# One language-model tower on one core: a copy moved to VectorE, a sum to GpSimd, and normalized rows transposed ahead of the scores

## The reference

```python
x = word_emb[ids] + pos_emb[arange(128)] + type_emb[types]
h = gamma * (x - mu) / sqrt(var + 1e-12) + beta
a = layernorm(h)                                   # eps 1e-5
q, k, v = a @ Wq, a @ Wk, a @ Wv                   # 16 heads of 16
q, k = head_layernorm(q), head_layernorm(k)        # with weight and bias
p = softmax(where(causal, q k^T / 4, -inf))
h = h + (p v) @ Wo + bo
x2 = layernorm(h)
score = softmax(x2 @ gate^T); top 2 of score + bias, the weight is the score
h = h + sum over the two: (silu(xw @ w1[e]) * (xw @ w3[e])) @ w2[e],  xw = x2 * score
```

## Time and profile before

| | |
|---|---|
| runs, median | 545.32 us |
| the profiled execution | 545.62 us |
| its span | 543.8 us |
| granted TensorE clock, mean | 0.992 of full speed |
| TensorE busy | 501.2 us (92%) |
| VectorE busy | 291.9 us (54%) |
| ScalarE busy | 250.7 us (46%) |
| GpSimd busy | 286.2 us (53%) |

### The profile page before, as it was taken

One profiled execution on the slowest core, in us unless ns is written; L12 is line 12 of the kernel. 1 busy time (PEld: TensorE's weight loads), 2 busy tenths in 40 slices (PEclk: granted clock), 3 DMA queues, 4 the chain that ended last, 5 costly groups with the idle time before them and its releaser, 6 DMA issues.

```text
span 543.8 us, 13452 instructions
## 1 busy us (share of the span) xinstructions
PE 501.2 (92%) x4470; PEld 428.7 (79%) x4471; DVE 291.9 (54%) x759; ACT 250.7 (46%) x575; POOL 286.2 (53%) x532
## 2 busy tenths in 40 slices
PE   5877989998999888999999999999999999999991
PEld 2345666777776665499999999999999999999980
DVE  2778888889989887733333333333333333333330
ACT  1166788978997883243223322332233323332320
POOL 4678787677764675214543454345434454344432
PEclk9999999999999999999999999999999999999996
DMA  5007721101028672302212221122112221222221
GB/s 174 10 22 243 231 85 31 58 29 29 29 80 278 212 251 84 90 22 41 29 30 39 39 39 22 37 39 39 23 36 39 39 28 31 39 38 30 30 39 19
DMA packets 29962, 36.75 MB, mean 68 GB/s; under 512 B 8272, under 2 KB 23504, under 8 KB 29936
## 3 DMA queue, kind: packets, MB, share of 16 engines
q0 software_dynamic: 8352, 12.76, 13.8%
q1 hardware_dynamic: 20768, 22.61, 13.1%
q10 hardware_dynamic: 816, 1.06, 0.6%
HBM read 26.81 MB, written 9.50 MB: 67 GB/s over the span
## 4 chain that ended last, share of the span: by engine, by line
PE 79%; DVE 5%; POOL 5%; ACT 4%; issue 3%; DMA 2%; POOLq 0%; DVEq 0%; ACTq 0%
PE PS L1445 35%; PE PS L1456 18%; PE PS L1172 10%; PE PS L1296 5%; PE PS L1254 2%; PE PS L1395 2%; PE PS L1271 2%; DMA x_pair<-word_dram,idx 1%; PE PS L1180 1%; ACT work L628 1%; PE PS L1310 1%; PE PS L1243 1%; DVE nmax L879 1%; DMA out_dram<-x_pair,dst_c 1%; POOL arena L477 1%
## 5 line engine op out<-in xcount | busy, mean ns | idle before, releaser
L1445 PEld LDWEIGHTS PS<-work,arena 128*128 128x128 f32 x1716 | 197.6, 192 | 2.3 <-ACT work L744 0.4
L1445 PE MATMUL PS<-work,arena 128*128 128x128 f32 x1716 | 198.0, 275 | 0.0
L750 ACT ACTIVATE work<-PS 128x768 f32<-128x768 f32 x39 | 31.6, 810 | 197.2 <-PE PS L1445 197.2
L1456 PE MATMUL PS<-w_sb,work 128*128 x468 | 107.6, 379 | 0.7 <-DVE x_pair L1147 0.7
L1139 DVE TENSOR_TENSOR work<-work,PS 128x640 f32<-128x640 f32 x39 | 32.0, 821 | 138.0 <-ACT work L750 138.0
L1456 PEld LDWEIGHTS PS<-w_sb,work 128*128 128x128 f32 x468 | 85.9, 190 | 11.2 <-issue 1.1
L572 POOL DMA_INDIRECT out_dram<-x_pair,dst_c x39 | 79.2, 2030 | 21.9 <-POOL dst_c L571 20.5
L571 POOL COPY dst_c<-dest_i 128x1 int32 (+1 forms) x39 | 7.1, 183 | 138.7 <-DVE x_pair L1147 136.5
L628 ACT ACTIVATE work<-PS,nmax 128x128 f32<-128x128 f32 x256 | 72.0, 401 | 3.7 <-DVE nmax L879 3.7
L740 ACT ACTIVATE arena<-w_sb 128x1408 f32 x40 | 55.1, 1379 | 12.0 <-DVE er_i L1115 9.0
L1172 PE MATMUL PS<-ident,work 128*128 128x128 f32 x336 | 54.8, 276 | 1.8 <-ACT work L628 1.8
(11 more groups left out here) (172 smaller groups left out, 618.8 us busy)
## 6 DMA issues: line engine op xcount, KB each, us to landing
w_sb<-w_dram SPq DMA_DIRECT2D x16, 640.0 KB, 5.6
w_sb<-w_dram SPq DMA_DIRECT2D x8, 704.0 KB, 4.5
x_rows<-x SPq DMA_DIRECT2D x16, 128.0 KB, 2.3
out_dram<-arena SPq DMA_DIRECT2D x16, 128.0 KB, 2.4
w_sb<-w_dram SPq DMA_DIRECT2D x16, 64.0 KB, 6.2
w_sb<-w_qkv_dram ACTq DMA_DIRECT2D x1, 768.0 KB, 8.2
work<-x_rows,src_c POOLq DMA_INDIRECT x41, 2.8
out_dram<-x_pair,dst_c POOLq DMA_INDIRECT x39
```

Source lines behind the costliest of these rows:

```text
L1445: last = n.matmul(up_ps[p][:, i, c, :], ws[p][:, k, at:at + P], xT_sb[p][:, k, :], start=(k == 0), stop=(k == DK - 1))
L1456: last = n.matmul(PS[:, 7, 0:D], hT_sb[p][:, i, :], w2_sb[:, bass.ds(e, 1), i, :], start=(i == 0), stop=(i == FK - 1))
```

## The change

- ScalarE's copy of the first bank of transposed probabilities goes to VectorE (`transposed_first`) for t of 2 and more, behind the keys. It has a semaphore of its own, `probsT0_ready`; those who wait for the copies wait for both.
- The sum of word rows and `x_base` goes from VectorE to GpSimd (`x_sum`) for sequences of 5 and more, ahead of the gather. VectorE's statistics of that sum move behind the `x2` normalization for t of 2 and more.
- The transposes of `a_n` for sequences of 4 and more go from behind the scores of the step t (for t + 2) to the end of the step (for t + 3), into the second half of VY_BANK, behind the mask banks and ahead of the next scores. ScalarE's copy `aT` goes to the end of its step. `outputs` waits for `aT` only at t = 1, and for `var_f` in each step.
- The keys of the sequences 0 to 2 are written by ScalarE, ahead of its queries, no longer by VectorE.

```diff
@@ gpsimd
+                def x_sum(u, q, n):
+                    pool.wait_ge(x_base_ready, u + 1)
+                    pool.wait_ge(gathered[q], 16 * (n + 1))
+                    g.tensor_tensor(x_in[q], x_in[q], x_base, ALU.add).then_inc(x_summed, 1)
+                    if valid(t + 4) and not at_step(t, 0):
+                        x_sum(t + 4, p, half(4))
                     if valid(t + 5):
                         gather(t + 5, 1 - p, link)
@@ scalar
                 def queries_out(u):
-                    act.wait_ge(k_ready, u + 1)
+                    if isinstance(u, int) and u < KEYS_BY_ACT:
+                        act.wait_ge(qk_ps, u + 1)
+                    else:
+                        act.wait_ge(k_ready, u + 1)
...
+                    if isinstance(u, int) and u < KEYS_BY_ACT:
+                        a.activation(kT.rearrange("p b s -> p (b s)"), PS[:, T_BANK, D:2 * D], ACT.Identity,
+                                     scale=cols_sb[:, 4:5], bias=cols_sb[:, 5:6]).then_inc(k_ready, 1)
                 u = t + 2
-                if valid(u):
+                if valid(u) and early_rows(u):
                     act.wait_ge(aT_ps, u + 1)
...
-                if valid(t):
+                if at_step(t, 1):
                     transposed(0)
...
                     transposed(3)
+                u = t + 3
+                if valid(u) and valid(t) and not early_rows(u):
+                    act.wait_ge(aT_ps, u + 1)
+                    act.wait_ge(v_done, u - 1)
+                    a.activation(aT[1 - p].rearrange("p k s -> p (k s)"), PS[:, VY_BANK, D:2 * D],
+                                 ACT.Copy).then_inc(aT_ready, 1)
@@ vector
+                def transposed_first():
+                    dve.wait_ge(probsT_ps, RG * t + 1)
+                    wait(dve, pv_done, t)
+                    v.tensor_copy(probsT[:, 0:512], PS[:, 0, :]).then_inc(probsT0_ready, 1)
...
                     keys_out(t + 1)
+                if valid(t) and not at_step(t, 0) and not at_step(t, 1):
+                    transposed_first()
...
-                if valid(t + 4) and valid(t):
+                if valid(t + 4) and valid(t) and (at_step(t, 0) or at_step(t, 1)):
                     sum_rows(t + 4, p, half(4))
...
                     normalize(x2[p][:, :], row(u), 2).then_inc(x2_ready, 1)
+                if valid(t + 4) and valid(t) and not at_step(t, 0) and not at_step(t, 1):
+                    sum_rows(t + 4, p, half(4))
@@ tensor
                 def outputs(u):
-                    pe.wait_ge(probsT_ready, RG * u + RG)
+                    pe.wait_ge(probsT0_ready, u + 1)
+                    pe.wait_ge(probsT_ready, (RG - 1) * u + RG - 1)
                     pe.wait_ge(v_ready, u + 1)
-                    wait(pe, aT_ready, u + 4)
+                    if at_step(t, 1):
+                        pe.wait_ge(aT_ready, u + 4)
...
                 u = t + 2
-                if valid(u):
+                if valid(u) and early_rows(u):
                     pe.wait_ge(a_ready, u + 1)
-                    wait(pe, var_f, u - 3)
                     wait(pe, aT_ready, u)
                     transposes(a_n, DK, O_BANK).then_inc(aT_ps, 1)
...
                     mask_banks(t + 1)
+                u = t + 3
+                if valid(u) and not early_rows(u):
+                    pe.wait_ge(a_ready, u + 1)
+                    pe.wait_ge(aT_ready, u)
+                    pe.wait_ge(v_ready, u - 1)
+                    transposes(a_n, DK, VY_BANK, D).then_inc(aT_ps, 1)
```

More of the change, by code:

```diff
@@ L224, in build_tower @@
         s_done, max_done, exp_done = sem("s_done"), sem("max_done"), sem("exp_done")
-        probsT_ps, probsT_ready, pv_done, o_ready = (
-            sem("probsT_ps"), sem("probsT_ready"), sem("pv_done"), sem("o_ready"))
+        probsT_ps, probsT_ready, probsT0_ready, pv_done, o_ready = (
+            sem("probsT_ps"), sem("probsT_ready"), sem("probsT0_ready"), sem("pv_done"), sem("o_ready"))
         o_raw_ready, o_back, oT_ps, oT_ready, wo_done = (
@@ L277, in build_tower, with early_rows @@
         EARLY = 5
+        KEYS_BY_ACT = 3
+        def early_rows(u):
+            return isinstance(u, int) and u < 4
         def valid(t):
@@ L634, in transposed @@
                     wait(act, pv_done, t)
-                    a.activation(probsT[:, r * 512:(r + 1) * 512], PS[:, T_BANK if r == RG - 1 else r, :], ACT.Copy).then_inc(probsT_ready, 1)
+                    a.activation(probsT[:, r * 512:(r + 1) * 512], PS[:, T_BANK if r == RG - 1 else r, :],
+                                 ACT.Copy).then_inc(probsT0_ready if r == 0 else probsT_ready, 1)
                 def x2_out(u):
@@ L684, in step @@
                     transposed(1)
+                    queries_out(1)
                     transposed(2)
-                    queries_out(1)
                     squares(2)
@@ L920, in sum_rows @@
                                                ALU.add).then_inc(x_base_ready, 1)
-                    dve.wait_ge(x_base_ready, u + 1)
-                    dve.wait_ge(gathered[q], 16 * (n + 1))
-                    v.tensor_tensor(x, x, x_base, ALU.add).then_inc(x_summed, 1)
+                    if isinstance(u, int) and u < EARLY:
+                        dve.wait_ge(x_base_ready, u + 1)
+                        dve.wait_ge(gathered[q], 16 * (n + 1))
+                        v.tensor_tensor(x, x, x_base, ALU.add).then_inc(x_summed, 1)
                     dve.wait_ge(x_summed, u + 1)
@@ L962, in step @@
                     normalize_a(2)
-                    keys_out(0)
                     squared_sums(1)
@@ L979, in step @@
                     first_norm(3)
-                    keys_out(1)
                     stats(link, row(3), 1, var_a)
@@ L1191, in rank @@
                     pe.wait_ge(v_ready, B - 2)
+                    pe.wait_ge(aT_ready, B)
                     n.matmul(ranks0, upper[:, :], chosen[:, s0:s1, :], start=True, stop=False, skip_group_check=True)
@@ L1235, in mask_banks @@
                     pe.wait_ge(exp_done, RG * u)
-                    pe.wait_ge(probsT_ready, RG * u - 1)
+                    pe.wait_ge(probsT0_ready, u)
+                    pe.wait_ge(probsT_ready, (RG - 1) * u - 1)
                     n.matmul(PS[:, RG - 2, 0:E], identb[:, :], mask[:, 0:E], start=True, stop=True)
@@ L1259, in outputs @@
                 def outputs(u):
-                    pe.wait_ge(probsT_ready, RG * u + RG)
+                    pe.wait_ge(probsT0_ready, u + 1)
+                    pe.wait_ge(probsT_ready, (RG - 1) * u + RG - 1)
                     pe.wait_ge(v_ready, u + 1)
-                    wait(pe, aT_ready, u + 4)
+                    if at_step(t, 1):
+                        pe.wait_ge(aT_ready, u + 4)
                     if at_step(t, B):
                         pe.wait_ge(added, 1)
-                    elif edge and t + 2 >= B:
+                    else:
                         wait(pe, var_f, u)
@@ L1346, in step @@
                     if not edge or t > 0:
-                        pe.wait_ge(probsT_ready, RG * t)
+                        pe.wait_ge(probsT_ready, (RG - 1) * t)
                     transposes(qkn, 2 * DK, T_BANK).then_inc(qk_ps, 1)
```

1 line of the change is left out of this document (removed).

## The result

The changed kernel takes 549.33 us (median of its runs, 548.15 to 549.48) against 545.38 us for the kernel before on the same chip (545.27 to 545.5): ratio 1.0065, 95% interval 1.0052 to 1.0078. It is slower by 3.9 us. The forecast was 546.4, 1.1 above the kernel before, with a range up to 548.8. So the sign of the forecast was right and its size was wrong. The profiled execution took 549.19 us, 3.57 more than the one of before.

What follows compares the result with a forecast made beforehand. TensorE's own work was taken to bound the steps, with VectorE's normalization late next. Terms 1.4 - 0.5 - 0.3 - 1.8 + 1.1 + 0.3 + 0.4 + 0.5 = +1.1 us gave 546.4; range 543.8 to 548.8.

Steps and rivals of the forecast that it cites:

- The old wait: TensorE idle ahead of `outputs` behind ScalarE's copy of the transposed rows, 0.65 us a step; the change takes it out.
- the head of a step: Scores to query transposes: gains only 0.09 us, not 0.65, because VectorE's normalization is late next; nine heads, -0.8.
- The even-odd difference that I put on `x2`: t = 5, 7, 9: transposes of `x2` start late behind VectorE; `x2` now comes earlier, 3 x 0.1, -0.3 us.
- The start: From t = -1: ScalarE makes the keys, VectorE's sum of squares starts at 29.85 instead of 31.71; -1.8 us.
- t = 1: GpSimd does its power before the sum, so VectorE's statistics start 1.12 later, ahead of the awaited division; +1.1 us.
- The issue-gap term: Scores of t = 5, 7, 9 after the loop's jump: queued transposes cover 0.15 us each, -0.5 in all.
- tails: Step ends: the two transposes behind the mask banks add their issue, 0.22 us each; ten tails, +2.2.
- The end: t = 12 and t = 14: VectorE has no idle time for the copy's 0.60 us; +0.4 and +0.5.
- Rival 2: Transposes at the step's end cost nothing, covered by mask banks and issue gap; 544.7 us; chance 0.25.
- Rival 3: The wait ahead of `outputs` goes as a whole, which needs a shorter query chain; 540 to 542 us; chance 0.1.
- Rival 1: GpSimd's sum holds VectorE, sign: statistics over 6.0 us behind the scores; +1.6, 548.0 us; chance 0.25.
- The 1.6 us that I worked out from it: t = 4 to 11: if sum and `x2` normalization exclude each other, TensorE waits 0.2 us in each step, +1.6.

Runs made afterwards that it cites:

- sum_back: The changed kernel with the sum of word rows and base row back on VectorE, where its statistics now stand: 550.05 us, ratio 1.0089 to the kernel before.
- after_hole: The changed kernel with the a_n transposes straight behind `outputs` and ScalarE's copy of them between the first and second exponentials: 547.25 us, ratio 1.0022 to the kernel before.
- copy_back: The changed kernel with the copy of the first bank back on ScalarE in all steps: 547.58 us, ratio 1.0035 to the kernel before.
- place_only: The kernel before with only the new place of the a_n transposes, behind the mask banks: 548.44 us, ratio 1.0055 to the kernel before.
- mix: after_hole with the first copy on ScalarE from t = 12 and the sum of t = 1 on VectorE: 545.44 us, ratio 0.9994 to the kernel before.
- keys_only: The kernel before with the keys of sequences 0 to 2 written by ScalarE, nothing else: 544.29 us, ratio 0.9975 to the kernel before.
- mix_order: mix with VectorE's normalization of queries and keys ahead of the second maxima: 545.89 us, ratio 1.0006 to the kernel before.

## Why the prediction was wrong in size

**What went as forecast.** The old wait goes and one for VectorE's normalization stands in its place; the head of a step gains 0.10 in the even steps and 0 in the odd ones (forecast 0.10 and 0.08, 0.09 on the mean). In the odd ones the chain of VectorE ends 3.05 us behind the scores in both kernels (135.41 + 0.68 less 133.04; 134.93 less 131.88), and TensorE follows 0.13 behind it, as before, not the 0.05 that I took. The even-odd difference that I put on `x2` is there (7.1 to 6.98). The start: the first scores come at 29.16 (forecast 29.2), and VectorE's sum of squares, by the rows of the kernel after, at 29.90 (forecast 29.85):

```profile
27.55 0.56 ACT L681 ACTIVATE w_sb<-PS,cols_sb 128x256 f32<-128x256 f32 x1 [1.64 <-PE PS L1205]
...
29.27 0.60 ACT L691 ACTIVATE w_sb<-PS 128x512 f32<-128x512 f32 x1 [0.24 <-PE PS L1333]
```

```profile
29.90 0.69 DVE L916 TENSOR_REDUCE ss<-w_sb 128x32 f32<-128x512 f32 x1 [0.15 <-ACT w_sb L691]
```

The scores of t = 1 come 1.76 earlier (39.73 in place of 41.49), forecast 1.8. At t = 1 VectorE waits for GpSimd's sum:

```profile
49.41 0.43 DVE L823 BATCH_NORM_STATS2 st<-x_pair 128x6 f32<-128x256 f32 x1 [2.75 <-POOL x_pair L481]
```

The statistics start 9.68 us behind that step's scores where they stood at 8.54 (50.03), 1.14 later, forecast 1.12. The step takes 1.52 more than before, forecast 1.1 and a tail of 0.22; sum_back gives 1.07 of it back. TensorE's wait for the division there, forecast at 1.8, is 1.7 us in after_hole; in the kernel after a slower projection lies over most of it (last section).

**The step that failed** is "the two transposes added behind the mask banks lengthen it by their issue: [...] I take 0.22". It is 0.37, inside the bound of 0.44, which I had left aside for the row nearest in kind. That row, 138.68 to 138.92 in the earlier trace rows, is of a pair among other full-array work. The row that stands at the place itself is the other one there, masks to scores, 142.28 to 142.64: 0.36 us, of which the weight load is busy for 0.12 (the row at 142.28 above) and pauses for the rest. So a pause was to be seen at that place, and by the runs there are two of them once the pair stands there. The issue-gap term itself held: of the 0.24 to 0.29 that the jump costs before, the pair hides 0.12 to 0.18, and I took 0.15; it only comes off 0.37. Over t = 4 to 11: tails 2.5 in place of 1.3 with the gap in it, heads -0.5 in place of -0.7, `x2` -0.4 in place of -0.3. These make 1.4 of the 2.5 us that the profiled sum is off.

**The end** is most of the rest, 0.7. I let t = 12 absorb its tail in the late division (+0.4 together). But the two lie one behind the other in TensorE's order: the division makes the middle of the step late, the tail its end, and the step is 0.85 longer, 0.59 for the copy (copy_back) and 0.26 for the rest. At the end the last maxima start 1.65 us behind the scores of t = 15 (201.25 against 199.60) where they stood at 1.19, which is the copy's doing too (copy_back has 1.19), and the experts start later by it. I had 0.5 for t = 14 and 15 together; t = 13 and 14 gave 0.14, and t = 15 gave 0.59. t = 2 and 3 are 0.14 over.

**The rivals.** Rival 2, a free tail, is refuted by place_only. Rival 3 is refuted by the wait of 9.2 us in ten steps: the query chain is as long as it was read. Rival 1 named a mechanism that is real and did not decide here: by its own sign the statistics would start more than 6.0 us behind the scores, and they start 5.54 behind them in t = 9 (138.58 against 133.04). In the kernel after the normalization of `x2` takes 0.41 us in seven of the steps t = 4 to 11, which there begins only near the end of GpSimd's addition (138.25, the addition of that step from 137.66 to 138.38); in after_hole and mix, where TensorE is faster, it takes 0.64 to 0.72 in every second one and 0.81 in t = 11, and the division comes late. I had argued that a one-input operation shows no faster mode and so would not be blocked. The rows refute that argument. By the Trainium skill (SBUF — State Buffer, "Who interferes with whom") a `tensor_scalar` can run in a 2-port mode, in which it and a GpSimd operation exclude each other. After_hole's rows agree as to the exclusion: 0.72 beside the addition against 0.41 without it. That the operation ran in such a mode no row shows; its 0.41 alone is hardly shorter than the 0.42 of an operation with two inputs. The 1.6 us that I worked out from it were not paid in the kernel after, whose 3.9 us have another cause.

## What to carry to other kernels

A wait that is taken away is worth only the distance to the chain that ends next; here that was 0.1 us of 0.65, and a second engine (VectorE) closed the step at two places, so that a gain at one came back as a wait at the other. Price an instruction by the rows at the place where it will stand, not by its likes elsewhere: between matmuls of unlike tile shapes the pair here cost 0.37 us and among its likes 0.22. Where a change has several parts, time them apart: here the placement alone loses 2.8 us, and the keys alone gain 1.3.

## What was not expected of the hardware

Where the tile shape of the matmuls changes, the next group starts 0.07 us ahead of the end of the one before, in place of 0.16. The busy times do not show it: the pair reads 0.44 us at the step's end and cost 0.37, and a pair among its likes reads 0.38 and cost 0.22. A pause of the weight load alone is not its mark, for from the first mask to the others (weight loads at 143.19, 0.10 long, and 143.31) the shape changes with 0.02 us of it, and inside the 512-column projection of that step it pauses 0.24 us with no change of shape.

In ten of the sixteen profiled executions TensorE ran at half clock for one or two stretches between 18 and 56 us. Granted clock and busy time of the kernel after, by stretches (us, busy us by engine, granted clock, DMA share, GB/s):

```profile
45.00:46.00 1.00, 1.00 (x6) 1.00 (x7) 0.88 (x1) 0.00 (x0) 1.00 (x3) 0.59 1.11 360
46.00:47.00 1.00, 1.00 (x5) 0.96 (x5) 0.61 (x2) 0.13 (x1) 0.89 (x2) 0.50 0.91 278
47.00:48.00 1.00, 1.00 (x2) 0.33 (x1) 0.00 (x0) 1.00 (x3) 0.92 (x3) 0.50 0.03 9
```

The projection of t = 1 in the kernel after and in after_hole, where the clock stayed at 1.00:

```profile
44.99 0.98 PE L1205 MATMUL PS<-ident,arena 128*128 128x128 f32 x4 [1.44 <-DVE arena L940]
...
46.62 2.86 PE L1333 MATMUL PS<-w_sb,front 128*128 128x512 f32 x4
```

```profile
45.46 1.88 PE L1334 MATMUL PS<-w_sb,front 128*128 128x512 f32 x4
```

At 0.50, the lower level of 1.2 GHz, it takes 2.86 in place of 1.88 us. Ahead of it TensorE had been idle for 0.55, 0.56 and 1.44 us; in after_hole it was idle at the same places for 0.56, 0.56 and 1.45 us, and the clock stayed. Whether the stretch comes, and where, differs between executions of nearly the same work: the kernel before, keys_only and place_only show none, mix has it in t = 0 (12.03 us there against 10.6 in after_hole). In the kernel after it costs little, since VectorE's late division covers it: t = 1 is 0.35 us longer than in after_hole, and the step's end accounts for 0.37. It may be behind the 1 to 3 us by which the runs of some variants spread. Of mix_order's twelve runs the fastest, 545.0 us, has a mean granted clock of 0.993 and the slowest, 548.25, of 0.982. That the stretches are the cause stays open, since single runs have no such rows.
